# Attention scores computed in two 64-row halves of the array, with early and later keys side by side and maximum rows per 512 queries

## What is computed

```python
ada = jax.nn.silu(c) @ W_ada + b_ada
shift_msa, scale_msa, gate_msa, shift_mlp, scale_mlp, gate_mlp = jnp.split(ada, 6, axis=-1)
h = _modulate(_layernorm(x), shift_msa, scale_msa)
# attention: per head, scores = (q * D ** -0.5) @ k.T over 2048 keys, softmax, times v
x = x + gate_msa * _attention(h, W_qkv, b_qkv, W_proj, b_proj)
h = _modulate(_layernorm(x), shift_mlp, scale_mlp)
mlp = jax.nn.gelu(h @ W_fc1 + b_fc1, approximate=True) @ W_fc2 + b_fc2
x = x + gate_mlp * mlp
```

## Time and profile before

| | |
|---|---|
| median of 3 runs | 3368.5 us (3368.29 to 3369.09) |
| the profiled execution | 3369.1 us, of which its span is 3367.4 us |
| granted TensorE clock in the span | 0.999 of full speed |
| TensorE busy | 3350.6 us |
| VectorE busy | 2000.6 us |
| ScalarE busy | 1523.8 us |
| GpSimd busy | 359.0 us |
| opening stage | to 423 us |
| attention stage | 423.6 to 2292.7 us |

### The profile page before, as it was taken

One profiled execution on the slowest core, in us unless ns is written; L12 is line 12 of the kernel. 1 busy time (PEld: TensorE's weight loads), 2 busy tenths in 40 slices (PEclk: granted clock), 3 DMA queues, 4 the chain that ended last, 5 costly groups with the idle time before them and its releaser, 6 DMA issues. The chain is left out here.

```text
span 3367.4 us, 45790 instructions
## 1 busy us (share of the span) xinstructions
PE 3350.6 (100%) x17032; PEld 2034.4 (60%) x17032; DVE 2000.6 (59%) x3591; ACT 1523.8 (45%) x2806; POOL 359.0 (11%) x283
## 2 busy tenths in 40 slices
PE   9999999999999999999999999999999999999999
PEld 7888833333333333333333333338989898898988
DVE  6447567777777777777777777745643332433332
ACT  3322366666656666655666666565531111211120
POOL 0000010111100000000000000025611101000000
PEclk9999999999999999999999999999999999999999
DMA  7563431312112121211212121116741212321211
GB/s 233 175 182 121 151 90 32 70 43 64 42 39 53 32 59 33 57 36 41 55 32 59 33 57 35 32 40 210 241 147 59 74 59 96 123 81 46 83 48 53
DMA packets 134722, 270.68 MB, mean 80 GB/s; under 512 B 18487, under 2 KB 40503, under 8 KB 127586
## 3 DMA queue, kind: packets, MB, share of 16 engines
q1 hardware_dynamic: 134502, 267.74, 28.5%
HBM read 169.21 MB, written 97.26 MB: 79 GB/s over the span
## 5 line engine op out<-in xcount | busy, mean ns | idle before, releaser
L1286 DVE TENSOR_REDUCE q_mx<-b_st 128x1 f32<-128x512 f32 x1968 | 1222.3, 684 | 487.6 <-PE b_st L1225 472.3
L1342 ACT ACTIVATE b_pt<-b_st 128x512 f32<-128x512 f32 x2048 | 1057.2, 603 | 586.3 <-PE b_st L1242 583.2
L1255 PE MATMUL b_op<-b_pt,b_vs 128*37 128x512 f32 x4096 | 981.8, 600 | 0.1
L1255 PEld LDWEIGHTS b_op<-b_pt,b_vs 128*37 128x37 f32 x4096 | 201.6, 113 | 486.6 <-ACT b_pt L1342 265.7
L2088 PE MATMUL d_pm<-d_vh,d_ah 128*128 128x288 f32 x1152 | 339.3, 295 | 2.2 <-DVE d_al L2126 2.2
L2089 PE MATMUL d_pm<-d_vl,d_ah 128*128 128x288 f32 x1152 | 339.3, 295 | 0.0
L2090 PE MATMUL d_pm<-d_vh,d_al 128*128 128x288 f32 x1152 | 339.2, 294 | 0.0
L1407 POOL TENSOR_TENSOR w_oc<-b_oa,b_ob 37x512 f32<-37x512 f32 x127 | 161.6, 1272 | 1533.4 <-DVE b_ob L1317 1527.7
L2088 PEld LDWEIGHTS d_pm<-d_vh,d_ah 128*128 128x128 f32 x1152 | 216.1, 188 | 3.3 <-issue 2.6
L1242 PEld LDWEIGHTS b_st<-q_qs,q_ks 110*128 110x128 f32 x704 | 118.5, 188 | 163.9 <-issue 119.7
L1242 PEld LDWEIGHTS b_st<-q_lo,q_hh 110*128 110x128 f32 x704 | 118.4, 188 | 162.9 <-issue 109.3
(11 more groups left out here) (416 smaller groups left out, 5062.7 us busy)
## 6 DMA issues: line engine op xcount, KB each, us to landing
qkh<-a_th SPq DMA_DIRECT2D x72, 256.0 KB, 2.0
qkl<-a_tl SPq DMA_DIRECT2D x72, 256.0 KB, 2.1
d_yi<-y SPq DMA_DIRECT2D x64, 288.0 KB, 3.0
n_oi<-hw SPq DMA_DIRECT2D x12, 1024.0 KB, 5.9
vd<-a_vx SPq DMA_DIRECT2D x8, 1184.0 KB, 6.5
b_vs<-vd SPq DMA_DIRECT2D x32, 296.0 KB, 6.9
a_x<-in_x SPq DMA_DIRECT2D x8, 1152.0 KB, 6.5
ot<-w_oc SPq DMA_DIRECT2D x128, 72.0 KB
```

Of the source, the lines that this page charges most:

```text
L1255: ins = e.matmul(op[64 * a:64 * a + VW, :], vs[h % 2][:, 2 * j + a, :], pt[g % NP][:, a * 512:a * 512 + 512], start=j == 0, stop=j == 7)
L1286: e.tensor_reduce(mx[:, k // 2, col:col + 1], bank(slots[a])[:, :], AX.X, ALU.max).then_inc(s_mx, 1)
L1342: e.activation(pt[g % NP][:, a * 512:a * 512 + 512], bank(k)[:, :], ACT.Exp, scale=SCALE).then_inc(s_p, 1)
```

## The change

The four parts, by the code:

- **Scores in halves.** A head's 110 rows are now held twice, in partitions 0 to 63 (with keys 0 to 1023) and 64 to 127 (with keys 1024 to 2047), as 64 rows in the tiles `qa` and `ka` and 46 rows (`ROWS`, with the two maximum rows at 44 and 45) in `qb` and `kb`. `scores_t` does key block j and key block 8 + j side by side: a matmul of 64 rows in each half, then one of 46 rows in each half that accumulates into the same bank. The maxima's matmuls read rows 0 to 35 of each half of `qa` and `ka`, so `km` is gone. A head is loaded with 16 DMAs in place of 9, into two sets (`NB = 2`), one head ahead instead of two. `pt` has 8 buffers instead of 6.
- **Order of a step.** One unit of maxima, the four scores, the other unit of maxima, then the products as before.
- **Maximum rows per 512 queries.** `row_max` and `max_rows` now work on 8 units (128 by 4 maxima) and are done four times a head, 127 times in the stage, the last matmul a plain one with 37 columns instead of a transpose with 16, and four DMAs in place of two each time. `THERE` is 16: the opening stage computes 16 units of the first head only, in two halves of 36 rows (32 matmuls in place of 80).
- **Evictions.** ScalarE evicts both parts of `op`.

```diff
@@ rows of a head
+def rows_a(q, k, h, l, q0, k0, t0):
+    for r in (0, 64):
+        keys = (t0 + r // 64 * LK, LK)
+        yield q, r, h, q0, D, t0, L
+        yield k, r, h, k0, D, *keys
+        yield q, r + D, l, q0, 64 - D, t0, L
+        yield k, r + D, h, k0, 64 - D, *keys
...
@@ phase_qkv
     def maxima(c, kind, n):
-        place = n + 4 if kind == "qk" else n
-        k = 26 * (c - HCH) + 2 * place - 18
-        if 0 <= k < 64:
-            return range(k, k + 2)
-        if c == NCH - 1 and place > 4:
-            return range(64 + 2 * (place - 5), 66 + 2 * (place - 5))
-        return range(0)
+        k = (NF + 4) * (c - HCH - 2) + (n + 4 if kind == "qk" else n)
+        return range(k, k + 1) if 0 <= k < 2 * UQ else range(0)
...
+            queries, keys = slice(qb * 128, qb * 128 + 128), slice(k * 512, k * 512 + 512)
+            for a in range(2):
+                r = slice(64 * a, 64 * a + D)
+                if n:
+                    e.wait_ge(s_mx, 2 * n - 1 + a)
+                e.matmul(sp[a][:, :], qs0[r, queries], ks0[r, keys], start=True, stop=True).then_inc(s_s, 1)
...
@@ phase_attention, plan
-    NB = 3
-    NP = 6
+    NB = 2
+    NP = 8
...
-    THERE = 40
+    THERE = 2 * UQ
...
-        s.late = plan[-1].last if plan else None
-        s.scores = [(x, use("st", x)) for x in range(4 * hb, 4 * hb + 4 if hb < NHB else 4 * hb)]
-        s.units = []
-        for _ in range(min(2 if hb else 0, 32 * NH - todo)):
-            m = 2 * (todo - THERE)
-            s.units.append((todo, use("mx", m), use("mx", m + 1)))
-            todo += 1
-            if todo % 32 == 0:
-                s.last = todo // 32 - 1
+        s.late = plan[-1].last if plan else 1
+        s.units, s.scores = [], []
+        for kind in ("mx", "st", "st", "mx"):
+            if kind == "st" and hb < NHB:
+                x = 4 * hb + 2 * len(s.scores)
+                s.scores.append((x, use("st", x), use("st", x + 1)))
+            elif kind == "mx" and todo < 32 * NH:
+                m = 2 * (todo - THERE)
+                s.units.append((todo, use("mx", m), use("mx", m + 1)))
+                todo += 1
+                if todo % UQ == 0:
+                    s.last = todo // UQ - 1
...
@@ SyncE
-            if h >= NB:
-                e.wait_ge(s_st, 64 * (h - 2))
+            if h == 1:
+                e.wait_ge(s_one, 1)
+            else:
+                e.wait_ge(s_st, 64 * (h - 1))
...
+        def max_rows(p):
+            h, u = divmod(p, 4)
+            for j, m in enumerate((mh, ml)):
+                e.wait_ge(s_mh, 2 * p - 1 + j)
+                for r in (ROWS - 2 + j, 64 + ROWS - 2 + j):
+                    e.dma_start(qb[h % NB][r:r + 1, u * 512:u * 512 + 512].bitcast(F), m[:, :].bitcast(F)).then_inc(
+                        s_m[h % NB], 16)
...
@@ TensorE
+        def max_rows(p, slot):
+            e.wait_ge(s_nm, p + 2)
             bank_free(e, slot)
-            e.transpose(bank(slot)[0:16, 0:128], nm[:, :], ident[:, :]).then_inc(s_mt, 1)
+            e.matmul(bank(slot)[0:VW, 0:128], nm[p % 2][:, :], ident[:, :], start=True, stop=True).then_inc(s_mt, 1)
...
+        def scores_t(x, *slots):
+            h, p, j = x // 64, x // 16, x % 16 // 2
             i = h % NB
+            if j == 0:
+                rows_there(e, p)
+            keys, queries = slice(j * 128, j * 128 + 128), slice(p % 4 * 512, p % 4 * 512 + 512)
+            for a in range(2):
+                r = slice(64 * a, 64 * a + 64)
+                bank_free(e, slots[a])
+                e.matmul(bank(slots[a])[:, :], ka[i][r, keys], qa[i][r, queries], start=True, stop=False)
+            for a in range(2):
+                r = slice(64 * a, 64 * a + ROWS)
+                e.matmul(bank(slots[a])[:, :], kb[i][r, keys], qb[i][r, queries], start=False, stop=True).then_inc(s_st, 1)
...
@@ VectorE
         def score_max(n, *slots):
-            k = n % 32
-            if k < 2:
-                e.wait_ge(s_nm, n // 32 - 1)
+            p, k = n // UQ, n % 32
+            if p > 4:
+                e.wait_ge(s_nm, p - 2)
             for a in range(2):
                 col = k % 2 * 2 + a
                 e.wait_ge(s_s, 2 * (n - THERE) + a + 1)
...
-                e.tensor_copy(ob[i][:, :], op[0:VW, :]).then_inc(s_oa, 1)
...
@@ ScalarE
                 e.activation(oa[i][:, :], op[64:64 + VW, :], ACT.Copy).then_inc(s_oa, 1)
+                e.activation(ob[i][:, :], op[0:VW, :], ACT.Copy).then_inc(s_oa, 1)
```

More of the change, by code:

```diff
@@ L1173, in sync @@
                 h, r = divmod(s.hb, 16)
-                if r == 0 and h + 2 < NH:
-                    load(h + 2)
+                if r == 0 and h + 1 < NH:
+                    load(h + 1)
                 if r == 4 and h + 1 < NH:
@@ L1211, in tensor, with score_max @@
     def tensor(e):
-        def score_max(n, ka, kb):
+        def score_max(n, *slots):
             h, k = divmod(n, 32)
-            qb, c, i = k // 2, k % 2, h % NB
-            queries, keys = slice(qb * 128, qb * 128 + 128), slice(c * 512, c * 512 + 512)
-            loaded(e, h)
-            if n == THERE:
-                e.wait_ge(s_one, 32)
-            bank_free(e, ka)
-            e.matmul(bank(ka)[:, :], qs[i][0:D, queries], ks[i][0:D, keys], start=True, stop=True).then_inc(s_s, 1)
-            bank_free(e, kb)
-            e.matmul(bank(kb)[:, :], qs[i][64:64 + D, queries], km[h % 2][64:64 + D, keys], start=True,
-                     stop=True).then_inc(s_s, 1)
@@ L1228, in max_rows @@
-        def max_rows(h, slot):
-            e.wait_ge(s_nm, h)
+            q, c, i = k // 2, k % 2, h % NB
+            queries, keys = slice(q * 128, q * 128 + 128), slice(c * 512, c * 512 + 512)
+            if k == 0:
+                loaded(e, h)
+            for a in range(2):
+                r = slice(64 * a, 64 * a + D)
+                bank_free(e, slots[a])
+                e.matmul(bank(slots[a])[:, :], qa[i][r, queries], ka[i][r, keys], start=True, stop=True).then_inc(s_s, 1)
+        def max_rows(p, slot):
+            e.wait_ge(s_nm, p + 2)
@@ L1265, in tensor @@
         for s in plan:
-            for x, slot in s.scores:
-                scores_t(x, slot)
-            for u in s.units:
+            for u in s.units[0:1]:
+                score_max(*u)
+            for x in s.scores:
+                scores_t(*x)
+            for u in s.units[1:2]:
                 score_max(*u)
@@ L1309, in select @@
                 e.tensor_copy(cols[r:r + H, C:640], who[:, 512:C]).then_inc(W.s_sel, 1)
+        for t in nm:
+            e.memset(t[:, :], 0.0).then_inc(s_nm, 1)
+        row_max(1)
         for s in plan:
[L1312 to L1317 removed]
             if s.hb == 0:
@@ L1350, in scalar @@
                 e.activation(oa[i][:, :], op[64:64 + VW, :], ACT.Copy).then_inc(s_oa, 1)
+                e.activation(ob[i][:, :], op[0:VW, :], ACT.Copy).then_inc(s_oa, 1)
             if s.hb == 0:
                 tile.evict(e)
-            for x, slot in s.scores:
-                exps(x, slot)
+            for x, *slots in s.scores:
+                for a in range(2):
+                    exps(x + a, slots[a])
             if s.block == INV + 1:
```

176 lines of the change are left out of this document (75 added, 101 removed).

## The result

The changed kernel takes 3409.2 us (median of 4 runs, 3409.1 to 3410.3) against 3368.8 us for the kernel before on the same chip: ratio 1.012, with a 95% interval of 1.010 to 1.014. It is 40 us slower; the forecast was 3388 us, 19 us slower, with a range of 3350 to 3417.

The account below looks back on a forecast made before the run. TensorE's own step time, 3.64 us with three changes of kind, was taken as the bound. Units +25.0, steps without units -32.7, maximum rows +46.6 - 12.1, opening -9.5, start +1.5: +18.8, giving 3388 us (range 3350 to 3417).

Parts of the forecast that it names:

- the maximum rows' own time: Attention stage: their matmul itself takes 0.14 us (0.03 to 0.35), beside 0.23 us of waiting; 0.37 us each, 126 times.
- The sum over the units: Attention stage: 502 steps with units at 3.61 us instead of 491 at 3.64, +25.0 us.
- The held step: Plain attention step: last maxima matmul waits for VectorE's first reduction until 1.45 us; step 3.61 us against 3.64.
- Opening stage: Opening stage: 80 matmuls go (18.8 us, about 1 us around them), 16 pairs come (10.1 us); net -9.5 us.
- Start: Attention stage's start: first reductions wait behind VectorE's part of the last q/k tile, +1.5 us (0 to 4).
- Steps without units, loads and ScalarE's evictions: Attention stage: 8 instead of 19 steps without units, at 2.97 us each, -32.7 us; loads and moved evictions cost nothing.
- What would show it: Signs: held matmul at 1.45 us, reduction at 0.60, steps 3.61 and 3.98, TensorE seen waiting for maxima in nearly every step.
- the view of waits: Sign: it would show TensorE waiting for VectorE's maxima in nearly every attention step.
- the one in which nothing is held: Rival, attention step: only the change of kind counts, last slot at 1.27 us; 3269 us, chance 0.05.
- the third: Rival, attention scores: accumulating halves don't run side by side, or row counts are different kinds; 3502 us, chance 0.07.
- the first: Rival, attention step: second semaphore costs VectorE nothing, reduction starts at 0.53 us; -35 us, 3353 us, chance 0.10.
- The fourth: Rival, attention stage: the maximum rows cost half as much, 23 us less, 3365 us; chance 0.08.

Follow-up runs that it names:

- half reductions: The changed kernel with VectorE's attention-stage maxima taken over 256 of each bank's 512 scores; 3293.2 us, ratio 0.977.
- the three runs with one pass: Changed kernel with the maximum rows' matmul as a transpose (3411.5 us) or in fp32r (3403.7 us); fp32r plus wait order, rows between products, later q/k part (3358.3 us).
- three edits together: Changed kernel with VectorE's waits swapped, maximum rows between the products, and VectorE's last q/k tile part after the first maxima; 3346.2 us, ratio 0.993.

## Why the prediction was right and wrong

The mechanism was right and the size was not: +40 us against a forecast of +19. The step that failed is the term for the maximum rows' own time: I had put 0.14 us, and it measured 0.21, which is 9 us of the 21 that are missing. The sum over the units makes 7 more, and the rest lies in the small terms below.

- **The held step: right.** 1.45 + 0.325 + 1.84, made of rows of before, gave 3.61 and the step is 3.62. The bank, the engine that reads it and both semaphores were as described, and halving the reduction gave the step without a hold.
- **The units' sum, 7 us too low.** I took 3.61 for all 502 steps. The plain step is 3.618 in the median, 4 us more (a rounding of 3.615 and 3 ns), and the mean is 3.633: ten long steps, one of them 6.11 us at 1485 us and four after 2270, add 7.5 us together, where the steps of before lay only 0.009 above the 3.64 that I used for them (4.4 us). In the step of 6.11 us VectorE computes a reciprocal for 3.33 us (from 1484.48) ahead of its reductions, TensorE waits 1.66 us for them, and from 1488 to 1492 us its granted clock is 0.76; the kernel before has one such step too, of 6.75 us at 1475 us. A sum over hundreds of steps wants the mean on both sides.
- **The maximum rows' own time, 9 us too low.** This is the term that was mis-sized most, and the step of the prediction that failed. I had put 0.14 us for a matmul of a quarter of the columns, with ends at 0.03 and 0.35; it is 0.21 (0.213 in the changed kernel, 0.209 with half reductions, 0.212 between the products). In the trace this plain fp32 matmul is two passes with two weight loads (248 records for 124 instructions), and the products' rows should have told me: eight records in a step for four matmul instructions. The 0.43 us of which I took a quarter is thus one pass of 512 columns in each column half, and two passes of 128 columns make 2 x 0.107 = 0.21. That the second pass is what was missing is this arithmetic and no experiment: the three runs with one pass also changed the kind of the matmul, and against two passes they saved 0.03 us, or lost 0.02 and 0.10. The 0.23 us of waiting was right (load at 2.00).
- **Opening stage, 1.3 us.** The 18.8 us of matmuls went and pairs came, and the net is 0.4 us off what was worked out; the other 0.9 us was already lost in the first 42 us of the run, where neither the diff nor the trace gives me a cause.
- **Start, 2 us too low, and right only in its sign.** Forecast was a wait behind the q/k tile's part, 1.5 us longer than today's. That wait is there (1.04 us at 418.08), but TensorE is idle for 2.4 us at this place in both kernels, so it adds nothing. Nearly all of the 3.6 us is a term that I had put at nothing: TensorE's granted clock falls there, as the last section shows.
- **Steps without units, loads and ScalarE's evictions: right.** -32.6 against -32.7; no wait for a head's load is seen, and none for the evictions beyond 0.4 us in total.
- **What would show it.** Of the signs that I had named, the held load, the reduction's start and the plain step came as given. Steps with the maximum rows take 4.06 us and not 3.98, and the view of waits did not show the hold: that sign was badly chosen, and alone it would have spoken against a theory that was right.
- **The rivals.** The held step's start leaves no room for the one in which nothing is held; the half reduction shows what it would have been worth, 0.166 us a step. The accumulating halves run side by side at 0.23 us a slot (1205.24, 1205.48, 1205.71, 1205.95), so the third falls. The second semaphore costs 0.07 us, so the first falls, and its price was right. The fourth had the maximum rows at half their cost; they cost more than forecast.

## What to carry to other kernels

When a change takes time from one engine, look at which buffer the last operation of the step uses, who reads it, and when that reader could start at the earliest; 0.07 us of a semaphore on the reader, 500 times, was 34 us of the 40 here. On an instruction with two waits, put the one that is met last first. Put a small matmul among matmuls of its own type and tiling, where its weights are loaded behind them, before trying to make it cheaper by itself.

## What I had not expected of the hardware

**Order of waits.** The same two semaphores on one VectorE instruction start it 0.60 us or 0.53 us after the matmul's start, by their order alone. This was run on VectorE only, and why the order matters no run shows.

**Change of kind by type.** 0.18 us to go from an fp32r matmul to fp32 products at the same tiling of 37 columns, with the unhidden weight load in it, and 0.310 us to go there and back, against 0.21 us for an fp32 matmul of two passes in the same places.

**The clock at the start.** The granted clock by stretch at the start of the attention stage, in the changed kernel (columns as above; the clock, as a share of full speed, is the third number from the end):

```profile
412.00:416.00 4.00, 2.67 (x15) 1.93 (x16) 1.00 (x4) 0.69 (x2) 0.64 (x1) 1.00 0.34 131
416.00:420.00 4.00, 2.88 (x16) 1.55 (x14) 3.26 (x6) 2.65 (x6) 3.78 (x5) 0.79 0.75 204
420.00:424.00 4.00, 4.00 (x18) 1.73 (x16) 2.77 (x6) 2.06 (x4) 1.91 (x3) 0.50 1.00 318
424.00:428.00 4.00, 4.00 (x22) 1.61 (x20) 2.00 (x4) 1.52 (x4) 2.17 (x2) 0.86 0.85 158
```

TensorE was idle for 1.3 us in the first of these and 1.1 us in the second; then, though it is busy from 420 on, it runs at 0.50, the 1.2 GHz level: the step that starts at 419.32 takes 6.15 us, where the next takes 3.55. That is 2.6 us of the start's 3.6; over the last three stretches the missing clock comes to an estimated 3.4 us (4 x 0.21 + 4 x 0.50 + 4 x 0.14). In the half reduction the clock stayed at 1.00 there, with 3.22 us busy in the second stretch, and the first two steps of the stage took 6.63 us, against 6.43 in the kernel before and 10.07 in the changed one.

The pauses alone do not decide it. The kernel before is idle there for 2.4 us at a clock of 1.00. With three edits together the second pause shrank (2.88 us busy became 3.81 of 4) and the clock fell all the same; in the run with scores first, the eviction on VectorE and the rows between the products it stayed at 1.00 with 3.72 us busy. What decides it is left open.
